# A decoder block on one Trainium2 core: second scores of one batch in the same slots as first scores of the next

## The reference

```python
# 1: linear attention, 32 heads of 8, relu on q, k, v
vk   = einsum('bnhe,bnhd->bhed', [v, 1], k)
out  = einsum('bhed,bnhd->bnhe', vk, q);  out[..., :D] / (out[..., D:] + EPS)
x = layernorm(x + out @ proj_weight.T + proj_bias)
# 2: cross attention on ctx, 16 heads of 16, rope in two dimensions, q and k rounded to float16
attn = softmax(rope(q) @ rope(k).T * 16 ** -0.5);  x = layernorm(x + (attn @ v) @ Wo.T + bo)
# 3: low-rank feed-forward, 256 -> 64 -> 1024 -> 64 -> 256
x = layernorm(x + gelu(x @ U1 @ V1 + b1) @ U2 @ V2 + b2)
```

## Time and profile before

| | us |
|---|---|
| median of 3 runs | 634.99 |
| lowest and highest run | 631.4, 635.81 |
| profiled execution, its own time | 636.95 |
| its span, first to last instruction | 635.0 |

### The profile page before, as it was taken

One profiled execution on the slowest core, in us unless ns is written; L12 is line 12 of the kernel. 1 busy time (PEld: TensorE's weight loads), 2 busy tenths in 40 slices (PEclk: granted clock), 3 DMA queues, 4 the chain that ended last, 5 costly groups with the idle time before them and its releaser, 6 DMA issues.

```text
span 635.0 us, 12707 instructions
## 1 busy us (share of the span) xinstructions
PE 555.6 (87%) x4288; PEld 369.3 (58%) x4288; DVE 464.2 (73%) x974; ACT 312.4 (49%) x455; POOL 286.8 (45%) x300
## 2 busy tenths in 40 slices
PE   0867799899999999999999999999996958999993
PEld 0755557575757575766657575757573524455561
DVE  4377569898988888889889798989887672244434
ACT  4321173645545463646373736455454626656561
POOL 3471535454546454637364554545453401224334
PEclk9886599999999999999999999999999877999998
DMA  7526200201020202020201111010000000033322
GB/s 251 124 69 131 64 6 10 67 9 67 8 66 8 66 8 67 7 70 11 66 18 58 39 35 63 11 66 8 34 9 18 26 1 17 18 106 121 104 99 100
DMA packets 24029, 33.77 MB, mean 53 GB/s; under 512 B 4552, under 2 KB 10440, under 8 KB 24008
## 3 DMA queue, kind: packets, MB, share of 16 engines
q1 hardware_dynamic: 23192, 33.07, 17.2%
q10 hardware_dynamic: 816, 0.43, 0.3%
HBM read 22.73 MB, written 8.65 MB: 49 GB/s over the span
## 4 chain that ended last, share of the span: by engine, by line
PE 61%; issue 10%; DVE 9%; ACT 8%; POOL 4%; POOLq 0%; DVEq 0%; ACTq 0%
PE FR L1013 14%; PE BK L1013 12%; PE BK L1174 9%; PE SC L1157 5%; DVE nmax L857 5%; PE SC L1133 5%; ACT probs L634 3%; PE FR L1081 3%; PE FR L1089 3%; PE FR L1071 3%; PE FR L1215 3%; PE BK L1185 2%; POOL rs L536 2%; POOL c_fm L541 2%; ACT x_fm L623 2%
## 5 line engine op out<-in xcount | busy, mean ns | idle before, releaser
L857 DVE TENSOR_REDUCE nmax<-SC 128x4 f32<-128x1024 f32 x128 | 149.8, 1216 | 12.4 <-PE SC L1133 12.3
L634 ACT ACTIVATE probs<-SC 128x1024 f32<-128x1024 f32 x128 | 124.3, 1033 | 19.5 <-PE SC L1157 19.5
L1174 PE MATMUL BK<-probs,v_aug 128*32 128x256 f32 x1024 | 69.5, 389 | 0.0
L1133 PE MATMUL SC<-k_blk,q_grp 32*128 32x512 f16 x256 | 49.2, 402 | 12.6 <-DVE nmax L857 12.6
L442 POOL TENSOR_TENSOR att_fm_l<-att_raw,att_fm_h 128x512 fp32r<-128x512 f32 x16 | 20.6, 1286 | 74.1 <-ACT att_raw L615 74.1
L1157 PE MATMUL SC<-q_grp,k_blk 64*128 64x256 f16 x512 | 45.9, 279 | 9.0 <-ACT probs L634 8.4
L696 ACT ACTIVATE probs<-SC,b_ff 128x512 f32<-128x512 f32 x64 | 39.6, 688 | 24.4 <-PE SC L1338 23.7
L431 POOL TENSOR_TENSOR k_cos<-k,cos_t 128x512 f16<-128x512 f16 x16 | 18.5, 1154 | 69.4 <-ACT k L591 69.4
L1174 PEld LDWEIGHTS BK<-probs,v_aug 128*32 128x32 f32 x1024 | 26.9, 110 | 28.2 <-issue 10.9
L838 DVE TENSOR_SCALAR x_tm<-y,mv,rs 128x256 f32<-128x256 f32 x32 | 39.1, 1261 | 3.9 <-POOL rs L447 3.9
L1157 PEld LDWEIGHTS SC<-q_grp,k_blk 64*128 64x128 f16 x512 | 17.5, 95 | 34.6 <-ACT probs L634 26.5
(11 more groups left out here) (173 smaller groups left out, 1623.0 us busy)
## 6 DMA issues: line engine op xcount, KB each, us to landing
x_fm<-in_x_fm SPq DMA_DIRECT2D x16, 256.0 KB, 2.7
x_tm<-in_x_tm SPq DMA_DIRECT2D x16, 256.0 KB, 2.9
c_fm<-in_c_fm SPq DMA_DIRECT2D x16, 256.0 KB, 3.4
x_kept<-x2b SPq DMA_DIRECT2D x16, 256.0 KB, 2.1
x_tm<-x_kept SPq DMA_DIRECT2D x16, 256.0 KB, 2.7
out<-c_fm SPq DMA_DIRECT2D x16, 256.0 KB, 2.0
k_blk<-k_rope SPq DMA_DIRECT2D x128, 16.0 KB, 1.8
cos_t<-rope_tables SPq DMA_DIRECT2D x1, 896.0 KB
```

The source lines that it names most:

```text
L634: act.activation(probs[:, j % 4], SC[j % 2][:], ACT.Exp, scale=SCALE).then_inc(s_exp, 1)
L857: dve.tensor_reduce(nmax[:, t, HC * q:HC * q + HC], SC[c % 2][:], AX.X, ALU.max, negate=True).then_inc(s_max, 1)
L1133: mm = pe.matmul(SC[c % 2][:, 2 * s:2 * s + 2].rearrange("p h t -> p (h t)"), q_grp[par][rows, q, t * P:(t + 1) * P], k_blk[par][rows, q]. ...
L1174: mm = pe.matmul(BK[q // 2][HP * k:HP * (k + 1), (q % 2) * T:(q % 2 + 1) * T], v_aug[par][:, t, HC * q + k], probs[:, j % 4, k], start=(t ...
```

## The change

A step now joins three neighbours differently. In step b, eight slots each hold one chunk of first scores and its row maximum for batch b+1, and one chunk of second scores and its exponential for batch b (slot 0 has the last chunk of batch b-1); in odd slots a pair of weighted sums follows. First scores have the buffer `SA`, second scores `SB`, one each. The linear attention belongs to batch b+3, its norm and q2 to b+2, o, att and wo to b-1, layer norm 2, x2's turn and the low-rank product to b-2. Step numbers begin at -3, and all steps are written out on every engine.

With it: `q_grp`, `k_blk`, `v_aug` and `x1b` have three buffers; the maxima and shift rows have another layout (first scores read 48 rows of each half, and the constants of `k_blk` come by DMA); `k_rope`, `xb_tm` and `att_tm` lose a buffer or go; norm1's two instructions and the copy of o's first half move from VectorE to ScalarE, with one small VectorE product in place; rope_q's last part (`rope_q_sum`) stands apart from the rest and is four instructions on 32 rows; the low-rank product is two matmul calls of 128 columns in place of four of 64; `shift_t` writes to `FR[0]`. The order of SyncE's start changes too: the large tables are asked for right behind the small part, ahead of the first `place_k` and of the x_fm load of batch 2.

The core of the diff (renamed arguments and index changes left out):

```diff
+SR = PR + D2
+NB = 3
...
-        shift_t16 = SC[0][:, 0].bitcast(F16)[:, 0:T]
+        SA, SB = SC
+        shift_t16 = FR[0][:].bitcast(F16)[:, 0:T]
...
             tables_in(0, 2 * T, s_tab_first)
-            sp.wait_ge(s_k_zeros, 2)
-            place_k(0, 0)
-            load_x(2, 0)
             tables_in(2 * T, B * T, s_tab_in)
...
+            for b in range(FIRST, B):
+                if b >= -2 and on(b + 4):
+                    load_x_fm(b + 4)
+                if b >= -1 and on(b + 3):
+                    load_c(b + 3)
+                if on(key_batch(b)):
+                    place_k(key_batch(b))
+                if on(b - 2):
+                    keep(b - 2)
+                if b >= -2 and on(b + 4):
+                    load_x_tm(b + 4)
```

The two score functions and their waits:

```diff
+            def scores1(n, c):
                 t, q = c // HC, c % HC
...
-                if c < 2:
-                    wait(pe, s_exp, NQ * b - 1 + c)
-                else:
-                    pe.wait_ge(s_max, NQ * b + c - 1)
+                wait(pe, s_max, NQ * n + c)
                 for s in range(2):
-                    rows = slice(TR * s, TR * s + PR)
-                    mm = pe.matmul(SC[c % 2][:, 2 * s:2 * s + 2].rearrange("p h t -> p (h t)"),
+                    rows = slice(TR * s, TR * s + SR)
+                    mm = pe.matmul(SA[:, 2 * s:2 * s + 2].rearrange("p h t -> p (h t)"),
...
+            def scores2(b, j):
                 q, t = j // 2, j % 2
                 if j == 0:
                     pe.wait_ge(s_shift_ev, 2 * b + 2)
-                if j < 2:
-                    pe.wait_ge(s_max, NQ * b + NQ - 1 + j)
-                else:
-                    pe.wait_ge(s_exp, NQ * b + j - 1)
+                wait(pe, s_exp, NQ * b + j)
```

More of the change, by code:

```diff
@@ L495, in _, with keep_x2, step @@
-            pool.sem_inc(s_x2b, 1)
+            def keep_x2(q):
+                pool.wait_ge(s_x2, 2 * q + 2)
+                wait(pool, s_x2_out, 16 * (q - 1))
+                pool.tensor_tensor(x2b[:, q % 2], x2_tm[:],
+                                   b_ff2[:].unsqueeze(1).broadcast_to([P, TT, C]), ALU.add).then_inc(s_x2b, 1)
+            def step(b):
+                n, m, p, q = b + 2, b + 3, b - 1, b - 2
+                if on(q):
+                    norm2(q)
+                if on(n):
+                    rstd1(n)
+                if on(m + 1):
+                    split_x(m + 1)
+                if on(p):
+                    att_lo(p)
+                if on(key_batch(b)):
+                    rope_k(key_batch(b))
+                if on(q):
+                    keep_x2(q)
+                if on(n):
+                    residual2(n)
+                if on(m):
+                    residual_bias(m)
+                if on(key_batch(b + 1)):
+                    split_c(key_batch(b + 1))
@@ L520, in _ @@
-            step(0, 0, 1, 1, 0, tail=False)
-            pool.wait_ge(s_tab_in, 32)
-            with pool.Fori(0, 6) as i:
-                step(2 * i + 1, i + 1, i + 2, i + 1, 1)
-                step(2 * i + 2, i + 1, i + 2, i + 2, 0)
-            step(B - 3, (B - 2) // 2, None, (B - 1) // 2, 1, linear=True)
-            step(B - 2, (B - 1) // 2, None, None, 0, linear=False)
-            step(LAST, None, None, None, 1, linear=False, cross=False)
+            for i in range(NB):
+                pool.memset(v_aug[i][:], 1.0).then_inc(s_v_ones, 1)
@@ L692, in _ @@
+            for b in range(FIRST, 0):
+                step(b)
+                if b == -3:
+                    for k in range(N_MAIN, len(split)):
+                        weights_hi(k)
+            for b in range(0, B):
+                step(b)
+            exp_chunk(LAST, 7)
+            ev_pv(LAST, 1)
             act.sem_inc(s_gelu, 4)
@@ L708, in _ @@
             ev_att(LAST)
-            for f in range(2, NF):
+            gelu(0, 2)
+            gelu(0, 3)
+            ev_x2t(LAST - 1)
+            gelu(0, 4)
+            ev_p(LAST - 1)
+            for f in range(5, NF):
                 gelu(0, f)
@@ L980, in _ @@
+            for b in range(FIRST, B):
+                step(b)
             dve.sem_inc(s_qf_ev, 1)
             dve.sem_inc(s_y3, 2)
+            stats2(LAST - 1)
             att_norm(LAST)
-            add2(LAST, 1)
+            add2(LAST)
+            ev_p(LAST - 1)
             stats2(LAST)
@@ L1066, in vk, with q1, kv1 @@
-            def vk(n):
-                pe.wait_ge(s_kv1_ev, 2 * n + 2)
+            def q1(m):
+                wait(pe, s_v2_ev, m if m < 3 else m - 1)
+                feature_major(BK[0], w_qkv1, 0, xs_fm).then_inc(s_q1_mm, 1)
+            def kv1(m, t):
+                if t == 0:
+                    pe.wait_ge(s_xs, m + 1)
+                    wait(pe, s_proj_ev, m)
+                elif m < 3:
+                    wait(pe, s_lint_ev, m)
+                if m == 0 and t == 0:
+                    pe.wait_ge(s_w_lo, 1)
+                product((FR[1], FR[0])[t][:], lambda i, c: xs_fm[i][:, c, t * P:(t + 1) * P],
+                        lambda i, c: w_qkv1[i][:, c, C:3 * C]).then_inc(s_kv1_mm, 1)
@@ L1327, in _ @@
+            for b in range(FIRST, B):
+                step(b)
+            scores2(LAST, 7)
+            pv(LAST, 6)
+            pv(LAST, 7)
             o_t(LAST, 1)
```

976 lines of the change are left out of this document (455 added, 521 removed).

## The result

The changed kernel takes 700.13 us (699.2 to 704.41), the kernel before beside it 633.19 us: a ratio of 1.107, interval [1.100, 1.114]. Forecast were 643 us and a range of 612 to 660. "Slower" was the likeliest direction by its chance, and the size is far outside. The profiled execution takes 699.2 us with a span of 697.4, so 62.4 us of span are to be found.

A forecast was written before the change was run, and what follows sets the result against it. Bound: a 30 us step, 28.1 of TensorE in order and 1.9 waiting. Start +6, first two steps -1, eleven full steps +7, end -6, last part +2: +8, 645 us profiled, 643 forecast, range 612 to 660.

The forecast's parts named there:

- TensorE's own work after the change: TensorE's matmul groups over the eight slots of a step: 27.15 us in sum, 0.9 less than before.
- The busy times of the other engines: Per full step: VectorE about 23.5 us, ScalarE 18, GpSimd staying at 15.5.
- Where the new step waits: In a full step, TensorE waits for lin before lin_t and for maximum 6 before slot 7: about 3.4 us of waits.
- The walk: One full step followed through all engines with profiled durations: 30.6 us, bounds 29.9 to 31.9; chance 0.53.
- I take 0.3, since only the tail of the last one meets it.: Per full step, rope_q's sum on VectorE meeting GpSimd's three additions: 0.3 us, bounds 0 to 1.4.
- rival b: GpSimd slips late and its additions cover rope_q's whole sum: steps of 34.5 us, 686 us in all; chance 0.10.
- The start: Up to the first shift transpose: 6 us later, bounds +3 and +9, with x_fm for batch 2 landing near 52.
- The end: Shift transpose 13 to the last weighted sum: 64.7 us for 70.8, so -6, give or take 4.
- The last part: Batch 14's low-rank product and turn move into the last part's first block: +2 us.
- Unrolling: Writing out all steps in place of a loop: costed at nothing.
- the first two steps: The two steps behind the first shift transpose: 27.5 + 29.0 us for 57.5 before, so -1.

The follow-up runs named there:

- e9_fill: Changed kernel with residual_bias behind split_x, residual2 opening the next step, p_ff ahead of wo, large tables later, 10 unused matmuls ahead of lin_t: 634.57 us.
- e1: Changed kernel with split_c moved ahead of residual2 and residual_bias in GpSimd's order: 660.42 us.
- e2: Changed kernel with thirty unused matmuls added ahead of lin_t, where TensorE waits: 677.18 us.
- e8: e1 with 14 unused matmuls added in the wait ahead of lin_t: 646.99 us, ratio 1.021.
- e4: Changed kernel with split_c ahead of the additions on GpSimd, and lin and maximum 6 ahead of rope_q's sum on VectorE: 690.97 us.
- e10: e9_fill without its 10 unused matmuls: 647.78 us.
- e12: e9_fill with 7 unused matmuls in place of 10, and rope_q's sum behind lin's copy before step 0 and from step 12 on: 627.53 us, ratio 0.989.
- e6: Changed kernel with residual_bias behind split_x, residual2 opening the next step, p_ff ahead of wo, and lin, maximum 6, lin's copy ahead of rope_q's sum: 644.75 us.
- e3: Changed kernel with lin and maximum 6 ahead of rope_q's sum in VectorE's order: 653.96 us.

## Why the prediction was wrong, by its own steps

**TensorE's own work after the change: right.** The sum was 27.15 us a step. In e9_fill, with the clock at 1.00, a step takes 29.35; less 1.2 for the ten matmuls, 0.3 ahead of lin_t and 0.5 ahead of the next score, 27.35 are left. The busy times of the other engines were right too: VectorE 24.1 us a step for 23.5, ScalarE 18.2 for 18.

**Where the new step waits: place right, size wrong.** The walk ended in lin_t behind lin and the first score behind maximum 6. The trace has the first of the two, 4.16 us; the second, 0.5 us, shows only in the experiments (e1, e2, e8, e9). The walk's 30.6 held a wait of about 3 us at both together. Without the collision and with the clock held (e8) the step is 29.7; the walk without its 0.3 for the collision had 30.3, so it was 0.6 too long.

**The step that failed: "I take 0.3, since only the tail of the last one meets it."** I let GpSimd run keep_x2, residual2 and residual_bias back to back from 19.1 to 23.0. residual2 can't: it waits for add2, which VectorE has just ahead of the sum. I had written down the test myself (rival b: "it decides from the moment that residual2 starts after 22"), and add2 ends after 22 in my own walk; I didn't lay GpSimd's waits over it. In the trace it starts 0.2 us after the sum's first instruction. The collision costs 2.3 us a step (4.0 for 1.7), about 2 more than counted. The page of before had the wait, 25.0 us of GpSimd's idle time released by add2 (L898 there), and its timeline had the collision in a full step: norm1's two instructions stand beside two GpSimd additions, and in 28 of 32 cases they take over 1 us where the shortest takes 0.40:

```profile
L453 POOL TENSOR_TENSOR x1b<-x_tm,b_o 128x512 f32<-128x512 f32 x16 | 21.5, 1343 | 25.8 <-DVE y L898 25.0
...
209.02 1.27 POOL L470 TENSOR_TENSOR x2b<-x_tm,b_ff 128x512 f32<-128x512 f32 x1
209.10 2.63 DVE L838 TENSOR_SCALAR x_tm<-y,mv,rs 128x256 f32<-128x256 f32 x2 [0.22 <-POOL rs L447]
...
210.25 1.33 POOL L424 TENSOR_TENSOR xb_tm<-x_tm,b_p 128x512 f32<-128x512 f32 x1
```

I took 1.35 for norm1's own price, and the one q_sin of 1.48 for a rare event.

By both of the signs that I had set for rival b, a step over 33 and a sum over 3, it is what came, with a chance of 0.10. Its mechanism was half right: the additions do cover the sum, but since add2 releases both, not since GpSimd slips late. Its step of 34.5 lies near the measured 34.0 by luck: +4.2 for the collision is nearly twice too high, and it left out the clock. The price was wrong in kind. I took 1.06 for each of four VectorE instructions; but each ends 0.27 to 0.28 us behind the GpSimd instruction that it meets, so there is one delay for each GpSimd instruction met, and the first one of the sum, which began ahead of residual2, had none. The upper bound of that step was short even by my own price: two such delays are 2.1 us and not 1.4.

The Trainium skill ("GPSIMD Engine Reference", Specifications) says that GpSimd's SBUF interface is shared with VectorE, with contention where VectorE has two SBUF inputs. The sum's instructions, two SBUF inputs each, agree: 1.39 to 1.42 for 0.42 where a GpSimd addition covers them (after, e4), and 0.40 to 0.42 beside an idle GpSimd (e1).

**A term that was missing: the clock.** The second step that failed, put at nothing without a reason. The walk priced every group of matmuls at the rate of a kernel that never waits long in its loop. The full-step rows had 1.00 throughout, but the rows of the start and the end had 0.68 and 0.83 next to idle time, and I had a wait of 3 us in every step of my walk. It costs 2.0 us a step (e2), and 1.4 where the gap is 1.46 (e9 and e10). Of the 44 us that eleven steps lose, 22 are this (e2 against the changed kernel), and 25.5 are the collision with the clock held (e2 against e8); without either, eleven steps are 3 us shorter than before. Walk, collision and clock: 30.6 + 2.0 + 2.0 = 34.6, less the 0.6 that the walk had too much: 34.0, as measured.

The Trainium skill ("TensorE: Matmul & The Clock Gate", Part 1) tells of the same two clocks and that activity releases the lower one. These runs agree in kind: 0.90 becomes 1.00 when matmuls of no use fill the gap.

**The start: +6 forecast, +15.8 measured.** That is outside the bounds of +3 and +9 as well. The x_fm of batch 2 had landed by 47.9 and not at 52, so my reason was wrong. What came late was something that I hadn't followed: GpSimd's rope_k(0) waits 8.76 us for the first sine table, residual_bias(0) stands behind it in order, and add1(0) waits for that until 38.02:

```profile
33.22 1.15 POOL L451 TENSOR_TENSOR k_cos<-k,cos_t 128x512 f16<-128x512 f16 x1 [8.76 <-DMA sin_t<-rope_tables]
...
36.66 1.26 POOL L440 TENSOR_TENSOR x_tm<-x_tm,b_p 128x512 f32<-128x512 f32 x1
...
38.02 0.69 DVE L862 TENSOR_TENSOR y<-FR,x_tm 128x512 f32<-128x512 f32 x1 [8.42 <-POOL x_tm L440]
```

Then the first sums collide (5.1 us for 1.7, one instruction at 2.47 where GpSimd splits a weight), lin(1) stands behind them, and add1(1) comes at 67.65. e12, which moves both out of the way (and asks for the large tables later, as e9 does, with its first shift transpose at 88.61), has its first shift transpose where the kernel before has it; its add1(0) runs at 31.11. How the 15.8 divide between the two, and how much of it is the 7 us that executions differ by, stays open.

**The end: -6 forecast, +0.6 measured.** I gave the three last steps 25, 20.5 and 19 us; they take 25.8, 24.0 and 21.5. In the middle one VectorE's copy of the low-rank product stands ahead of maximum 5 and waits 4.4 us for ScalarE, and TensorE waits 5.1 us for maxima in four pieces. With p_ff ahead of wo (e6, e9) and what else these change, that step takes 20.3. The first two of the three together take 49.9 us, and 45.1 in e6, 46.5 in e9, but also 46.3 in e4, where wo still stands first, so which edit gives it wasn't told apart. The last part was +1.5 for +2.

**Unrolling and the first two steps.** Unrolling costs nothing that the runs show: the steps of e8 and e9, all written out, are shorter than the loop's. The first two steps take 57.7 us where 56.5 were forecast and 57.5 stood before, 1.2 us off. In the sum for the end the three steps of 25, 20.5 and 19 make 64.5 and not 64.7, which changes nothing.

## What to carry to other kernels

Before pricing one engine's run of instructions, lay the other engine's run over it with its waits in it: a wait that is released by the instruction ahead of the sensitive one sets both off together, every time. Look in the profile of before for what the other engine's run collides with now: if that is moved away, it can meet something else. Price an idle gap of TensorE twice, for its length and for the slower matmuls behind it, above all when the gap stands just ahead of the slot that everything waits for. And when two edits each part a collision, check that they don't shift both sides alike.

## What the runs showed of the hardware that wasn't expected

A kernel gets faster by doing more: thirty matmuls a step that nobody reads took 700 us to 677, ten took 648 to 635, with the order of every other engine as it was. TensorE's clock fell to 1.2 GHz behind gaps as short as 1.46 us, in ten of e10's eleven steps, but not behind each: of eleven equal gaps of 1.85 us in e1, seven were followed by it and four not, and the step is 29.5 to 29.7 us, 30.8 to 31.2 or 32.5 by that alone. In the loop of the changed kernel, behind a gap of 4.16, it came in every step and lasted for most of the 6.9 us that follow.

A 32x512 f16 addition of 0.42 us on VectorE takes 1.40 to 1.42 beside a GpSimd addition, which itself is stretched little (L440 takes 1.44 for 1.26). The price isn't a factor: in all thirteen profiles with the split sum, every one of its instructions that took over 0.6 us ended 0.26 to 0.28 us behind the end of the GpSimd instruction that it met. So it is as dear as what is left of that one: 0.74 beside a tensor_scalar of 0.78, 2.47 at the start beside a weight's subtraction of 2.52. VectorE's row maximum and lin, beside the same additions in e3, weren't slowed.
